# A graph layer whose adjacency is built by one-hot products: steps of one chunk instead of two, with the one-hots made on GpSimd

## The chip, the cores and the metric

One core of one Trainium2 chip runs the whole program. The metric is the device time of one execution in microseconds, as the median of the runs shown. Engines are named as in the profile: PE multiplies matrices, DVE is the vector engine, ACT the scalar engine, POOL GpSimd, SP the engine that issues DMAs.

## What is computed

x has 3125 nodes of 256 features, with 100000 edges sorted by destination. A graph attention layer and a mixture of experts follow each other, each with a residual:

```python
h = layernorm(x); q, k, v = h @ wq + bq, h @ wk + bk, h @ wv + bv
scores = sum(q[dst] * k[src], -1) / 16 + edge_weight * we + be
exp_s = exp(scores - segment_max(scores, dst)[dst])
attn = exp_s / segment_sum(exp_s, dst)[dst]
out = segment_sum(v[src] * attn[:, None], dst)
y = layernorm(h + out + h @ ws + bs) * g1 + b1
x = x + layernorm(y + gelu(y @ w_ff1 + b_ff1) @ w_ff2 + b_ff2) * g2 + b2
e = argmax(layernorm(x) @ router_w.T + router_b)         # 32 experts, 64 hidden units
x = x + relu(relu(layernorm(x) @ W1[e] + b1[e]) @ W2[e] + b2[e])
```

## The kernel before, in words

Attention is computed densely: for each tile of 125 destinations, scores against all sources, masked and weighted by an adjacency matrix A[destination, source] of summed exp(edge weight) factors. So most of the first half of the program builds A in DRAM (`adj`).

**Preparation.** 98 partitions hold 1024 edges each. DVE turns the edge weights into guarded exponents, counts at which steps each window of 5 destinations (`WIN`) begins (L989 to L991 per block of 128 steps, L1016 to L1018 per block of windows) and writes per edge a code (destination and source block, L1002) and three terms of the source's place in its block (L1003 to L1008). SP stores the last step of each window (`last_lin`, L475) and, behind that in its program, the table of edges (`edge_tab`, L484); POOL gathers the table's rows step by step (L598) and fills two rows of ones (L602); DVE makes the codes relative to their window (L1026), PE and ACT turn codes and values so that an edge of the step stands in each partition (`code_tab`, `nval_tab`, L1333 to L1341 and L757 to L765), SP stores the terms (L489) and loads them back as rows (L494). Meanwhile PE and ACT compute k, q, v and the skip part of all nodes (L1294 to L1313, L710 to L738).

**The adjacency loop** runs over 1015 steps, rounded up to 1024: 512 groups (`NG`) of 2 steps (`GROUP`), each step of 2 chunks (`SUB`) of 128 edges, all of one window; `turns` (L406) unrolls 16 groups (`BODY`) and repeats them 32 times. Per chunk, with an edge in each partition:

- PE computes the distance of the edge's place to each of 128 columns as a product of 5 bf16 rows (`distances`, L1349): (column - place) squared, less 1.
- ACT takes relu(-value x that) out of PSUM (`columns`, L778), which is the value where the column is the edge's place and 0 elsewhere (`Ys`).
- DVE compares a row of 0..124 with the code (`one_hot`, L1053), which gives for each edge a one-hot over 5 destinations x 25 source blocks (`Xs`), one instruction for two chunks.
- PE multiplies one-hot by columns (`product`, L1363, matmul at L1371, fp32), the 2 chunks of a step adding up in PSUM: a block of A of 125 x 128. An fp32 product has two records in the profile.
- DVE adds the block to the sum so far, which `keep_tab` multiplies by 1 inside a window and by 0 where one begins (`sums`, L1065, at L1081), into one of 4 buffers (`STAGES`) of `stage`. Between two add-ups stands the one-hot of a later group (L1085).
- SP stores the group's two sums to `adj` (`put`, L523), and once in 8 groups zeros to `xs_dram` (L517) and a load of the next distance rows (L495).

PE takes, per group, first the distances of two groups later, then the products. Buffers of `Xs`, `Ys` and `stage` are reused after four groups; an add-up waits for the store of four groups before (L1069).

POOL stands outside of the loop: it waits until the stores of the first tiles' rows have landed (L615) and gathers the rows of A for tiles 0 and 1 (`fetch`, L617) while the loop still runs; the others follow after it, one per tile.

**Attention**, 25 tiles: DVE turns zeros of A into a mask (`exclude`, L1104), PE computes scores in 7 blocks of columns (`front`, L1380; three fp32r products for each half of the 256 features), DVE adds the mask and takes the maximum (`guard`, L1112), ACT takes the exponent (L793), DVE multiplies by A (`weigh`, L1122), PE transposes 25 blocks and multiplies by v (`back`, L1396). The rest (FFN, routing, experts) isn't touched.

## Time and profile before

| | us |
|---|---|
| median of 3 runs | 1892.36 |
| the runs | 1892.36, 1878.16, 1903.58 |
| span of the profiled execution, first to last instruction | 1885.6 |
| busy in the span: PE, DVE, ACT, POOL | 1656.9 (88%), 1193.9 (63%), 965.5 (51%), 300.8 (16%) |

The profiled execution's time is known by its span alone; the median of the runs lies 6.8 us above it. A group of the profile is a set of instructions of one line, engine and shape, with its count, its busy time in us and the mean of one in ns, and after the second bar the idle time of the engine just before them, with what ended it. A mean of instructions that overlap is longer than the distance between their starts, so rates are read from the timeline. In a row of the chain or of the timeline the first number is the start in us and the second the duration; SPq is SP's DMA queue.

### The profile page before, as it was taken

How to read it: one execution, taken by the hardware profiler on the slowest of the kernel's cores; microseconds unless marked ns; L12 is line 12 of the kernel's file. 1: busy time of each engine (PE TensorE's matmuls, PEld its weight loads, DVE VectorE, ACT ScalarE, POOL GpSimd, SP SyncE). 2: the span in 40 equal slices, each digit the busy share in tenths (PEclk: the TensorE clock that was granted, in tenths of full speed). 3: DMA queues.
4: the chain of work that ended last, by engine and by line, in shares of the span. 5: the costliest groups of instructions: out<-in, count | busy, mean ns of one | idle time of the engine just before them, and what ended most of it. 6: DMA issues, size and time to landing. Idle time of an engine off the chain costs nothing.

```text
span 1885.6 us, 41069 instructions
## 1 busy us (share of the span) xinstructions
PE 1656.9 (88%) x11015; PEld 1378.6 (73%) x11015; DVE 1193.9 (63%) x3327; ACT 965.5 (51%) x2962; POOL 300.8 (16%) x397
## 2 busy tenths in 40 slices
PE   2898999999799999999899999999999789419960
PEld 1796888888688888887688888888888779315640
DVE  3927898988688889898555555555555578701111
ACT  1566888888588888887233333333333345103210
POOL 0022000000000000000111111111110067375435
PEclk9999999999899999999999999999999889656555
DMA  6054333333433333334822222222210100047634
GB/s 159 28 129 115 104 105 104 106 103 105 140 104 104 106 105 103 104 105 112 164 76 77 76 76 76 76 78 75 76 75 37 53 17 0 6 117 214 181 113 121
DMA packets 226999, 180.40 MB, mean 96 GB/s; under 512 B 41884, under 2 KB 218038, under 8 KB 223544
## 3 DMA queue, kind: packets, MB, share of 16 engines
q1 hardware_dynamic: 189327, 112.46, 21.6%
q0 software_dynamic: 21408, 61.20, 9.7%
q10 hardware_dynamic: 16224, 6.27, 1.5%
q8 instruction: 17, 0.28, 0.1%
q14 instruction: 23, 0.19, 0.0%
HBM read 84.94 MB, written 99.11 MB: 98 GB/s over the span
## 4 chain that ended last, share of the span: by engine, by line
PE 78%; DVE 6%; DMA 5%; POOL 4%; issue 3%; SPq 2%; ACT 1%; POOLq 0%; DVEq 0%; ACTq 0%
PE bank L1371 29%; PE bank L1404 15%; PE bank L1392 11%; PE bank L1356 9%; PE bank L1411 3%; PE bank L1486 3%; PE bank L1493 2%; PE bank L1478 2%; PE bank L1444 2%; PE bank L1436 2%; POOL arena L691 2%; POOL xs_dram L669 2%; SPq L458 1%; DMA V<-in_x 1%; DMA arena<-in_x 1%
## 5 line engine op out<-in xcount | busy, mean ns | idle before, releaser
L784 ACT ACTIVATE arena<-bank,tables 128x128 f32<-128x128 f32 x2048 | 585.2, 369 | 144.5 <-PE bank L1356 144.4
L1371 PE MATMUL bank<-arena 128*125 128x128 f32 x4096 | 585.9, 286 | 11.8 <-DVE arena L1055 11.8
L1371 PEld LDWEIGHTS bank<-arena 128*125 128x125 f32 x4096 | 488.4, 188 | 65.1 <-DVE arena L1055 11.9
L1055 DVE TENSOR_TENSOR arena<-iota_row,tables 128x250 f32<-128x250 f32 x1024 | 421.1, 412 | 0.1
L1081 DVE SCALAR_TENSOR_TENSOR arena<-arena,tables,bank 125x128 f32<-125x128 f32 x1023 | 351.9, 344 | 86.5 <-PE bank L1371 37.1
L1404 PE MATMUL bank<-V,arena 125*125 125x256 f32 x1250 | 296.4, 382 | 5.6 <-ACT arena L810 5.6
L810 ACT COPY arena<-bank 125x500 f32<-125x500 f32 (+1 forms) x175 | 90.8, 533 | 379.5 <-PE bank L1411 379.5
L1404 PEld LDWEIGHTS bank<-V,arena 125*125 125x125 f32 x1250 | 223.3, 188 | 38.0 <-ACT arena L810 10.3
L1122 DVE CUSTOM_DVE_ANT_0 arena<-arena 125x3200 f32<-125x3200 f32 x25 | 87.3, 3493 | 222.2 <-ACT arena L793 222.2
L622 POOL COPY gidx<-arow 125x1 uint32 (+1 forms) x25 | 36.4, 1455 | 1182.2 <-DVE wk_sb L1122 856.7
L1356 PE MATMUL bank<-dist_rhs,arena 5*128 5x128 bf16 x2048 | 201.6, 218 | 4.2 <-DVE tables L1039 3.4
L1356 PEld LDWEIGHTS bank<-dist_rhs,arena 5*128 5x128 bf16 x2048 | 113.8, 93 | 66.3 <-issue 4.0
L1392 PE MATMUL bank<-k_hi,q_hi 128*125 128x512 f32 (+1 forms) x350 | 137.7, 393 | 10.3 <-DVE wk_sb L1112 6.9
L1392 PE MATMUL bank<-k_lo,q_hi 128*125 128x512 f32 (+1 forms) x350 | 133.2, 380 | 0.0
L1392 PE MATMUL bank<-k_hi,q_lo 128*125 128x512 f32 (+1 forms) x350 | 133.2, 380 | 0.0
L1112 DVE CUSTOM_DVE_ANT_0 arena<-bank,arena 125x512 f32<-125x512 f32 (+1 forms) x175 | 103.0, 631 | 28.0 <-PE bank L1392 19.1
L793 ACT ACTIVATE arena<-arena,wk_sb 125x512 f32<-125x512 f32 (+1 forms) x175 | 115.8, 679 | 9.6 <-DVE wk_sb L1117 9.6
L1271 DVE TENSOR_SCALAR arena<-bank 128x256 f32<-128x256 f32 x56 | 23.7, 424 | 152.7 <-PE bank L1493 152.7
L1411 PE MATMUL bank<-ident,arena 125*125 125x125 f32 x625 | 94.5, 276 | 2.7 <-issue 2.7
L1411 PEld LDWEIGHTS bank<-ident,arena 125*125 125x125 f32 x625 | 88.7, 190 | 9.4 <-issue 3.1
L1392 PEld LDWEIGHTS bank<-k_hi,q_hi 128*125 128x125 f32 x350 | 65.9, 188 | 30.5 <-DVE wk_sb L1112 13.2
L1478 PE MATMUL bank<-ident,V 128*128 128x128 f32 x112 | 37.2, 434 | 55.1 <-DMA V<-xs_dram 55.1
(219 smaller groups left out, 1665.5 us busy)
## 6 DMA issues: line engine op xcount, KB each, us to landing
adj<-arena SPq DMA_DIRECT2D x512, 125.0 KB
xs_dram<-zeros SPq DMA_DIRECT2D x64, 112.0 KB, 3.2
V<-xs_dram SPq DMA_DIRECT2D x56, 128.0 KB, 2.3
ys_dram<-arena SPq DMA_DIRECT2D x56, 128.0 KB, 1.9
w_dram<-in_L_ffn_W SPq DMA_DIRECT2D x2, 2048.0 KB
V<-in_x SPq DMA_DIRECT2D x5, 625.0 KB
q_dram<-arena ACTq DMA_DIRECT2D x25, 125.0 KB, 2.3
wq_sb<-q_dram SPq DMA_DIRECT2D x25, 125.0 KB, 7.8
```

Source lines behind the costliest of these rows:

```text
L784: ins = nc.scalar.activation(Ys[:, q, k, :], bank[2 + s][:, k * LO:(k + 1) * LO], ACT.Relu, scale=nval_tab[:, bass.ds(i, 1)])
L793: ins = nc.scalar.activation(Z[0:TILE, s, c:c + n], Z[0:TILE, s, c:c + n], ACT.Exp, bias=nmax[:, s:s + 1])
L810: nc.scalar.copy(PT[0:TILE, s, j:j + n, :], bank[4 + g % 2][0:TILE, 0:n * TILE].rearrange("p (n d) -> p n d", n=n)).then_inc(pt_ready, 1)
L1055: ins = V_.tensor_tensor(Xs[:, s, cols, :], iota_row[:, 0:TILE].unsqueeze(1).to_broadcast([P, SUB, TILE]), code_tab[:, bass.ds(g * GC + k ...
L1081: ins = V_.scalar_tensor_tensor(stage[0:TILE, q, k, :], prev, keep_tab[0:TILE, bass.ds(g * GROUP + k, 1)], ps, ALU.mult, ALU.add)
L1112: V_.tensor_tensor_reduce(out=Z[0:TILE, s, c:c + n], in0=bank[b % 4][0:TILE, 0:n], in1=Z[0:TILE, s, c:c + n], scale=1.0, scalar=-BIG, op0= ...
L1122: V_.tensor_tensor_reduce(out=Z[0:TILE, s, :], in0=Z[0:TILE, s, :], in1=A_sb[0:TILE, s, :], scale=1.0, scalar=0.0, op0=ALU.mult, op1=ALU.a ...
L1356: ins = mm(bank[2 + s][:, k * LO:(k + 1) * LO], dist_rows[:, j // LOADG, c:c + CHUNK], dist_rhs[:, :], start=True, stop=True)
L1371: ins = mm(o, Xs[:, j % STAGES, k, :], Ys[:, j % STAGES, k, :], start=(k % SUB == 0), stop=(k % SUB == SUB - 1))
L1392: ins = mm(bank[b % 4][0:TILE, 0:n], q[:, s, k, :], v[:, k, j, :].rearrange("p j l -> p (j l)"), start=(i == 0), stop=(i == len(parts) - 1))
L1404: ins = mm(bank[6 + s][0:TILE, 0:D], PT[0:TILE, s, j, :], V[:, j, :], start=(j == 0), stop=(j == NT - 1))
L1411: ins = tr(bank[4 + g % 2][0:TILE, j * TILE:(j + 1) * TILE], Z[0:TILE, s, (j0 + j) * LO:(j0 + j) * LO + TILE], ident[0:TILE, 0:TILE])
```

## The change

`SUB` goes from 2 to 1: a step has one chunk, so there are 1406 steps, rounded up to 1408, in 704 groups of 2 steps (44 turns of 16), and a product is complete after one matmul. The tables in preparation grow with it: 11 blocks of 128 steps for 8 (`SBLK`), 784 columns for 392 in the counts (`NS`), one gather per block for two.

A source is now block x 131 + place: 24 blocks of 131 places (`HI`, `LO`) instead of 25 of 128 columns with 125 used. The one-hot has 120 columns, a block of A is 120 x 131, its row 3144 numbers, and scores are computed in 7 blocks of 448 columns.

The two distance products of a group take their 5 rows from different strips of 32 partitions (`STRIP`), into different banks (`dist_bank`); the rows are loaded by two DMAs, and two fills of POOL write the ones.

The one-hots are made by POOL, one tensor_scalar per chunk with the code as a scalar per partition, from copies of 16 codes (`held`); only the last group of every eight (`OWN`) is made by DVE in one instruction. POOL's gathers for attention stand behind its whole loop. PE's wait for the sums of four groups earlier, which lay in the order of DVE's instructions before, is now written out.

The core of the diff:

```diff
-SUB = 2
+SUB = 1
...
-LO = 128
-ROW = NT * LO
+HI, LO = 24, 131
+ROW = HI * LO
+MW = WIN * HI
+KB = 448
+NCOL = 7 * KB
 DIST = 5
+STRIP = 32
...
-ZROWS = MT * P // (2 * TURNS)
+ZROWS = -(-MT * P // (2 * TURNS * 12)) * 12
...
-SCH = [(c, min(512, ROW - c)) for c in range(0, ROW, 512)]
+SCH = [(c, KB) for c in range(0, NCOL, KB)]
...
-        with nc.sbuf_tensor("kT", [P, KH, NT, LO], F32) as kT, nc.sbuf_tensor("tables", [P, KH * ROW], F32) as tables:
+        with nc.sbuf_tensor("kT", [P, KH, NCOL], F32) as kT, nc.sbuf_tensor("tables", [P, KH * NCOL], F32) as tables:
...
-        Xs = view(STAGES * GC * TILE).rearrange("p (s k m) -> p s k m", s=STAGES, k=GC)
+        Xs = view(STAGES * GC * MW).rearrange("p (s k m) -> p s k m", s=STAGES, k=GC)
...
+        HELD = LOADG * GC
+        LOADW = LOADG * CHUNK
+        dist_rows = view(LOADW)[0:(GC - 1) * STRIP + DIST, :].bitcast(BF16).rearrange("p (s c) -> p s c", s=2)
...
+        OWN = LOADG - 1
+        def pool_groups(j, i):
+            return i * (BODY - 2) + j - j // LOADG
+        def dist_bank(s, k):
+            return bank[2 + s + 4 * k]
...
-                sp.dma_start(dist_rows[2:DIST, s, :], term_rows.ap().rearrange("c i e -> c (i e)")[
-                    :, bass.ds(n * LOADW, LOADW)]).then_inc(rows_in[s], 16)
+                for k in range(GC):
+                    sp.dma_start(dist_rows[k * STRIP + 2:k * STRIP + DIST, s, :].rearrange("c (i e) -> c i e", e=CHUNK),
+                                 term_rows.ap().rearrange("c (i k) e -> c k i e", k=GC)[
+                                     :, k, bass.ds(n * LOADG, LOADG), :]).then_inc(rows_in[s], 16)
...
-                             stage[0:TILE, j % STAGES, :, :]).then_inc(stored[j % STAGES], 16)
+                             stage[0:MW, j % STAGES, :, :]).then_inc(stored[j % STAGES], 16)
...
-            nc.gpsimd.memset(dist_rows[0:2, :, :], 1.0).then_inc(ones_set, 1)
+                        bass.IndirectOffsetOnAxis(ap=cidx[:, u, b:b + 1], axis=0)).then_inc(gath_in[b // 2], 16)
+            pool.wait_ge(ws_set, KH + 1)
+            for k in range(GC):
+                if k:
+                    pool.wait_ge(ones_set, k)
+                nc.gpsimd.memset(dist_rows[k * STRIP:k * STRIP + 2, :, :], 1.0).then_inc(ones_set, 1)
...
+            pool.wait_ge(ones_set, GC)
+            pool.wait_ge(tab_set, SBLK)
+            pool.wait_ge(terms_stored, 16 * SUB * SBLK)
+            def hold_codes(n, h):
+                nc.gpsimd.tensor_copy(held[:, h, :], code_tab[:, bass.ds(n * HELD, HELD)]).then_inc(codes_held, 1)
+            hold_codes(0, 0)
+            def one_hots(g, j, i):
+                h = j // LOADG
+                if j % LOADG == 0:
+                    pool.wait_ge(codes_held, 2 * i + h + 1)
+                if j % LOADG == 2 and not (isinstance(i, int) and i == TURNS - 1 and h):
+                    wait_from(pool, x_ready, pool_groups(j, i) - 2)
+                    hold_codes(2 * i + h + 1, 1 - h)
+                if j % LOADG == OWN:
+                    return
+                wait_from(pool, prod_done, g - STAGES + 1)
+                pool.sem_inc(pool_mark, 1)
+                for k in range(GC):
+                    c = j % LOADG * GC + k
+                    ins = nc.gpsimd.tensor_scalar(Xs[:, j % STAGES, k, :], iota_row[:, 0:MW], held[:, h, c:c + 1], None,
+                                                  ALU.is_equal)
+                ins.then_inc(x_ready, 1)
+            turns(pool, one_hots)
...
-                    ins = nc.scalar.activation(Ys[:, q, k, :], bank[2 + s][:, k * LO:(k + 1) * LO], ACT.Relu,
+                    ins = nc.scalar.activation(Ys[:, q, k, :], dist_bank(s, k)[:, 0:LO], ACT.Relu,
...
-            od(V_.scalar_tensor_tensor(codes_o, chunked(dstf), float(NT), chunked(hi_e[:, 0:EROW]), ALU.mult, ALU.add))
-            od(V_.scalar_tensor_tensor(srcf, hi_e[:, 0:EROW], -float(TILE), srcf, ALU.mult, ALU.add))
+            rounded(hi_e[:, 0:EROW], srcf, 1.0 / LO, 0.5 / LO - 0.5)
+            od(V_.scalar_tensor_tensor(codes_o, chunked(dstf), float(HI), chunked(hi_e[:, 0:EROW]), ALU.mult, ALU.add))
...
-            def one_hot(g, s, k):
-                cols = slice(k * SUB, (k + 1) * SUB)
-                ins = V_.tensor_tensor(Xs[:, s, cols, :], iota_row[:, 0:TILE].unsqueeze(1).to_broadcast([P, SUB, TILE]),
-                                       code_tab[:, bass.ds(g * GC + k * SUB, SUB)].unsqueeze(2).to_broadcast([P, SUB, TILE]),
-                                       ALU.is_equal)
-                if k == GROUP - 1:
-                    ins.then_inc(x_ready, 1)
-            for g in range(STAGES - 1):
-                for k in range(GROUP):
-                    one_hot(g, g, k)
...
-                    prev = stage[0:TILE, q, k - 1, :] if k else stage[0:TILE, (q - 1) % STAGES, GROUP - 1, :]
-                    ps = product_bank(j)[0:TILE, k * LO:(k + 1) * LO]
+                    prev = stage[0:MW, q, k - 1, :] if k else stage[0:MW, (q - 1) % STAGES, GROUP - 1, :]
+                    ps = product_bank(j)[0:MW, k * LO:(k + 1) * LO]
                     if first:
-                        ins = V_.tensor_copy(stage[0:TILE, q, k, :], ps)
+                        ins = V_.tensor_copy(stage[0:MW, q, k, :], ps)
                     else:
-                        ins = V_.scalar_tensor_tensor(stage[0:TILE, q, k, :], prev,
-                                                      keep_tab[0:TILE, bass.ds(g * GROUP + k, 1)], ps, ALU.mult, ALU.add)
+                        ins = V_.scalar_tensor_tensor(stage[0:MW, q, k, :], prev,
+                                                      keep_tab[0:MW, bass.ds(g * GROUP + k, 1)], ps, ALU.mult, ALU.add)
                     ins.then_inc(sum_ord if k < GROUP - 1 else sums_ready, 1)
-                    if not (isinstance(i, int) and i == TURNS - 1 and j > BODY - STAGES):
-                        one_hot(g + STAGES - 1, (q - 1) % STAGES, k)
+                if j % LOADG == OWN - STAGES + 1:
+                    V_.tensor_tensor(Xs[:, OWN % STAGES, :, :], iota_row[:, 0:MW].unsqueeze(1).to_broadcast([P, GC, MW]),
+                                     code_tab[:, bass.ds((g + STAGES - 1) * GC, GC)].unsqueeze(2).to_broadcast([P, GC, MW]),
+                                     ALU.is_equal).then_inc(own_x_ready, 1)
...
-                mm(bank[0][:, 0:NS], ones[0:PP, :], s_diag, start=True, stop=True).then_inc(rows_bc, 1)
+                mm(bank[0][:, 0:512], ones[0:PP, :], s_diag[:, 0:512], start=True, stop=True)
+                mm(bank[1][:, 0:NS - 512], ones[0:PP, :], s_diag[:, 512:NS], start=True, stop=True).then_inc(rows_bc, 1)
...
-                    pe.wait_ge(rows_in[j // LOADG], 16 * loads)
+                    pe.wait_ge(rows_in[j // LOADG], 16 * GC * loads)
+                c = j % LOADG * CHUNK
                 for k in range(GC):
-                    c = ((j % LOADG) * GC + k) * CHUNK
-                    ins = mm(bank[2 + s][:, k * LO:(k + 1) * LO], dist_rows[:, j // LOADG, c:c + CHUNK], dist_rhs[:, :],
+                    rows_ = slice(k * STRIP, k * STRIP + DIST)
+                    ins = mm(dist_bank(s, k)[:, 0:LO], dist_rows[rows_, j // LOADG, c:c + CHUNK], dist_rhs[rows_, :],
...
-                pe.wait_ge(x_ready, g + 1)
+                if j % LOADG == OWN:
+                    pe.wait_ge(own_x_ready, 2 * i + j // LOADG + 1)
+                else:
+                    pe.wait_ge(x_ready, pool_groups(j, i) + 1)
+                wait_from(pe, sums_ready, g - STAGES + 1)
+                wait_from(pe, sums_ready, g - STAGES + 1)
                 for k in range(GC):
-                    o = product_bank(j)[0:TILE, k // SUB * LO:(k // SUB + 1) * LO]
+                    o = product_bank(j)[0:MW, k // SUB * LO:(k // SUB + 1) * LO]
...
-                        ins = mm(bank[b % 4][0:TILE, 0:n], q[:, s, k, :], v[:, k, j, :].rearrange("p j l -> p (j l)"),
+                        ins = mm(bank[b % 4][0:TILE, 0:n], q[:, s, k, :], v[:, k, c:c + n],
```

## Rows read from the trace of the kernel before

**Rows 1.** Stages: us; PE, PEld, DVE, ACT, POOL busy; granted clock, DMA share, GB/s.

```profile
158.60:889.40 730.80, 716.54 (x6136) 601.45 (x6136) 640.92 (x2047) 585.64 (x2048) 3.25 (x4) 0.99 0.37 106
889.40:1484.00 594.60, 577.15 (x2925) 489.44 (x2925) 317.41 (x699) 202.67 (x379) 63.74 (x46) 0.99 0.25 78
...
1640.00:1885.00 245.00, 132.65 (x448) 81.66 (x448) 39.17 (x70) 41.18 (x112) 128.56 (x162) 0.53 0.50 145
```

**Rows 2.** Timeline of one period of the loop; start us, us, engine, operation.

```profile
700.12 0.39 PE L1356 MATMUL bank<-dist_rhs,arena 5*128 5x128 bf16 x4
...
700.45 1.14 PE L1371 MATMUL bank<-arena 128*125 128x128 f32 x8
700.53 0.35 DVE L1081 SCALAR_TENSOR_TENSOR arena<-arena,tables,bank 125x128 f32<-125x128 f32 x1 [0.30 <-PE bank L1371]
...
700.79 0.41 DVE L1055 TENSOR_TENSOR arena<-iota_row,tables 128x250 f32<-128x250 f32 x1
701.12 0.34 DVE L1081 SCALAR_TENSOR_TENSOR arena<-arena,tables,bank 125x128 f32<-125x128 f32 x1
...
701.52 0.39 PE L1356 MATMUL bank<-dist_rhs,arena 5*128 5x128 bf16 x4
```

**Rows 3.** DVE groups: adding up, one-hot, and two that wait on the one before.

```profile
L1055 DVE TENSOR_TENSOR arena<-iota_row,tables 128x250 f32<-128x250 f32 x1024 | 421.1, 412 | 0.1
L1081 DVE SCALAR_TENSOR_TENSOR arena<-arena,tables,bank 125x128 f32<-125x128 f32 x1023 | 351.9, 344 | 86.5 <-PE bank L1371 37.1 <-DMA adj<-arena 14.7
...
L1131 DVE RECIPROCAL wk_sb<-wk_sb 125x1 f32<-125x1 f32 x25 | 4.1, 164 | 0.9
```

**Rows 4.** POOL: groups by shape, and one instruction of its timeline.

```profile
L650 POOL TENSOR_TENSOR wk_sb<-wk_sb,minus_half 125x1 f32<-125x1 f32 x50 | 29.5, 589 | 9.2 <-POOL wk_sb L647 9.2
...
L589 POOL TENSOR_TENSOR ws_sb<-ws_sb,ident 128x128 f32<-128x128 f32 x2 | 0.9, 454 | 14.1 <-DMA bq_col<-in_L_gnn_bq 14.1
...
L590 POOL TENSOR_SCALAR_AFFINE_SELECT before<-before 128x128 f32<-128x128 f32 x1 | 0.3, 294 | 0.0
...
1543.17 0.22 POOL L647 TENSOR_SCALAR wk_sb<-wk_sb 125x1 f32<-125x1 f32 x1
```

**Rows 5.** The store of one group: its issue, its transfer's window, and another store's landing.

```profile
162.48 5.46 SPq L523 DMA_DIRECT2D adj<-arena  x4
...
163.30:164.90 1.60, 1.60 (x15) 1.37 (x15) 0.98 (x4) 0.66 (x3) 0.00 (x0) 0.92 0.29 80
...
ys_dram<-arena SPq DMA_DIRECT2D x56, 128.0 KB, 1.9
```

**Rows 6.** The stall in the loop: the chain, and the gather on POOL before it.

```profile
481.65 17.52 DMA adj<-arena
...
479.26 1.47 POOL L625 DMA_INDIRECT arena<-adj,gidx  x1 [1.00 <-POOL gidx L622]
```

**Rows 7.** Preparation: timelines of DVE and of SP's queue, and POOL's gathers as a group.

```profile
75.46 0.43 DVE L990 TENSOR_SCALAR arena<-arena,step_col 128x392 f32<-128x392 f32 x1
75.92 0.56 DVE L991 TENSOR_REDUCE cnt<-arena 128x1 f32<-128x392 f32 x1
...
103.74 0.26 SPq L475 DMA_DIRECT2D last_lin<-wrow  x1
...
146.95 5.86 DVE L1026 TENSOR_SCALAR arena<-arena,wneg 128x256 f32<-128x256 f32 x2 [2.27 <-DMA arena<-edge_tab,cidx]
...
L598 POOL DMA_INDIRECT arena<-edge_tab,cidx x16 | 15.5, 969 | 111.8 <-DMA edge_tab<-arena 107.2 <-issue 4.6
```

**Rows 8.** The turn into attention: POOL's gathers, DVE's first masking, one front.

```profile
arena<-adj,gidx POOLq DMA_INDIRECT x25, 15.8
...
896.41 1.82 DVE L1104 TENSOR_SCALAR arena<-arena 125x3200 f32<-125x3200 f32 x1
...
1118.47 9.02 PE bank L1392 x42
```

**Rows 9.** PE at the other clock, at the start of the loop.

```profile
162.00 1.88 PE L1371 MATMUL bank<-arena 128*125 128x128 f32 x8
```

More of the change, by code:

```diff
@@ L153, in gnn_moe @@
         x1 = sb("x1", [TILE, NT, D])
-        ARENA = 19050
+        ARENA = 19260
         arena = sb("arena", [P, ARENA])
@@ L176, in gnn_moe @@
         assert SBLK * SUB * TABW <= edges_only
-        cmp_o = view(4 * P)
-        s_row, o_row, iota_c = view(4 * P), view(4 * P), view(4 * P)
-        cmp_s, s_row, o_row, iota_c = (v[:, 0:NS] for v in (cmp_o, s_row, o_row, iota_c))
+        cmp_o = view(NS)
+        s_row, o_row, iota_c = view(NS), view(NS), view(NS)
+        cmp_s = cmp_o
         diag_flat = view(SBLK * P)
@@ L295, in gnn_moe @@
             "code_set", "idx_set", "rel_set", "tabT_done", "tab_set", "keep_set"))
-        gath_in = [sem(f"gath_in{b}") for b in range(SBLK)]
+        s_copied, codes_held, own_x_ready = sem("s_copied"), sem("codes_held"), sem("own_x_ready")
+        gath_in = [sem(f"gath_in{b}") for b in range(-(-SBLK // 2))]
+        gathered = [16 * min(2, SBLK - 2 * b) for b in range(-(-SBLK // 2))]
         last_set, last_stored, last_in, arow_set = (sem(n) for n in ("last_set", "last_stored", "last_in", "arow_set"))
@@ L329, in gnn_moe @@
         x_t = x.rearrange("(t p) d -> p t d", p=TILE)
-        xs_v, ys_v = (v.ap().rearrange("(j p) d -> p j d", p=P) for v in (xs_dram, ys_dram))
+        xs_v, ys_v = (v.ap()[0:MT * P, :].rearrange("(j p) d -> p j d", p=P) for v in (xs_dram, ys_dram))
         out_t = out.rearrange("(t p) d -> p t d", p=TILE)
@@ L609, in _ @@
             pool.wait_ge(q_stored[1], 16 * (NT // 2))
+            pool.wait_ge(ones_set, GC)
[15 more added lines that the diff above has]
+                pool.sem_inc(pool_mark, 1)
+                for k in range(GC):
+                    c = j % LOADG * GC + k
[3 more added lines that the diff above has]
+            turns(pool, one_hots)
             last_group = (2 * TILE // WIN + NS - 2) // GROUP
@@ L799, in key_parts @@
                 c, n = SCH[b]
-                j = slice(c // LO, (c + n) // LO)
-                nc.scalar.copy(k_hi[:, :, j, :], kT[:, :, j, :]).then_inc(k_hi_set, 1)
+                nc.scalar.copy(k_hi[:, :, c:c + n], kT[:, :, c:c + n]).then_inc(k_hi_set, 1)
             def weights(t, s, t_next, u):
@@ L939, in _ @@
             i1 = iota_row[0:1, :]
-            od(V_.tensor_tensor(cmp_o[0:1, 0:P], i1, i1, ALU.mult))
-            rounded(cmp_o[0:1, P:2 * P], cmp_o[0:1, 0:P], 1.0 / P, 0.0)
-            od(V_.tensor_scalar_mul(dist_line[:, 0, :], cmp_o[0:1, P:2 * P], float(P)))
-            od(V_.scalar_tensor_tensor(dist_line[:, 1, :], cmp_o[0:1, 0:P], -1.0, dist_line[:, 0, :], ALU.add, ALU.subtract))
+            lo_sq, lo_sqh = cmp_o[0:1, 0:LO], cmp_o[0:1, LO:2 * LO]
+            od(V_.tensor_tensor(lo_sq, i1, i1, ALU.mult))
+            rounded(lo_sqh, lo_sq, 1.0 / P, 0.0)
+            od(V_.tensor_scalar_mul(dist_line[:, 0, :], lo_sqh, float(P)))
+            od(V_.scalar_tensor_tensor(dist_line[:, 1, :], lo_sq, -1.0, dist_line[:, 0, :], ALU.add, ALU.subtract))
             od(V_.tensor_copy(dist_line[:, 2, :], i1))
@@ L996, in _ @@
             od(V_.tensor_tensor(wneg[:, :], cnt[:, :], step_col[:, :], ALU.subtract))
[L997 removed]
+            od(V_.tensor_scalar_mul(wneg[:, :], wneg[:, :], float(WIN * HI)))
             chunked = lambda ap: ap.rearrange("p (k e) -> p k e", k=PC)
             od(V_.tensor_copy(srcf, si))
[L1001 to L1003 removed]
+            rounded(hi_e[:, 0:EROW], srcf, 1.0 / LO, 0.5 / LO - 0.5)
+            od(V_.scalar_tensor_tensor(codes_o, chunked(dstf), float(HI), chunked(hi_e[:, 0:EROW]), ALU.mult, ALU.add))
+            od(V_.scalar_tensor_tensor(srcf, hi_e[:, 0:EROW], -float(LO), srcf, ALU.mult, ALU.add))
             od(V_.tensor_scalar_mul(terms_o[:, :, 0, :], chunked(srcf), -2.0))
@@ L1095, in key_rest @@
                 c, n = SCH[b]
-                j = slice(c // LO, (c + n) // LO)
                 dve.wait_ge(k_hi_set, b + 1)
-                V_.tensor_tensor(k_lo[:, :, j, :], kT[:, :, j, :], k_hi[:, :, j, :].bitcast(F32), ALU.subtract).then_inc(k_split, 1)
+                V_.tensor_tensor(k_lo[:, :, c:c + n], kT[:, :, c:c + n], k_hi[:, :, c:c + n].bitcast(F32),
+                                 ALU.subtract).then_inc(k_split, 1)
             def exclude(t, s, u):
@@ L1103, in exclude @@
                 wait_from(dve, tr_ready, len(TRG) * (t - 1))
-                V_.tensor_scalar(Z[0:TILE, s, :], A_sb[0:TILE, s, :], 0.0, -BIG, ALU.is_equal, ALU.mult).then_inc(excluded, 1)
+                V_.tensor_scalar(Z[0:TILE, s, :], A_sb[0:TILE, s, 0:NCOL], 0.0, -BIG, ALU.is_equal, ALU.mult).then_inc(excluded, 1)
             def guard(t, s, u):
```

56 lines of the change are left out of this document (27 added, 29 removed).

## The prediction

> **What bounds the kernel now.** I read the page first, then the busy time by stage. The adjacency loop (from 158.6 to 889.4 us) is the largest stage with 730.8 us, in which PE is busy for 716.5, DVE for 640.9, ACT for 585.6 and POOL for 3.3; attention follows with 594.6, and what comes after it takes 1885.6 - 1484.0 = 401.6 us [rows 1]. The change rebuilds the loop, so I then read one period of it. PE starts distances at 700.12 and again at 701.52: 1.39 to 1.40 us per group, with nothing between PE's pieces. Four distances take 0.33 (0.082 each) and eight product records 1.06 (0.133 each; a product has two records). DVE starts an add-up, a one-hot 0.26 later and the next add-up 0.33 after that, so its two pairs need 1.18 of the 1.39: PE bounds the loop, and DVE hides its waits behind one-hots [rows 2]. 512 x 1.392 = 713 us; the other 18 are one stall of 17.5 us, after POOL's gathers for the first attention tiles had started inside the loop and the stores of the loop waited for the same DMA engines [rows 6].
>
> **The loop after.** A chunk of 128 edges is now a step of its own: ceil(100000/128) + 624 = 1406 steps instead of 1015, rounded up to 704 groups of 2 chunks where there were 512 groups of 4. I cost one group on every engine.
>
> PE: 2 products are 4 records of 0.133 (131 columns for 128 add about 2%, 120 rows of weights for 125 take something off) = 0.53; 2 distances at 0.082 = 0.16, or about 0.10 if the two row strips run beside each other, which no row shows. 0.63 to 0.70, I take 0.69 [rows 2]. That is 486 us against 713: PE is no longer what is late.
>
> DVE: it still adds up twice, each add-up reading the sum before it. An add-up takes 0.344 [rows 3]. So far a one-hot stood between two of them; now the second comes at once and waits for the first. The nearest row of an instruction that waits for the one just before on DVE idles 0.9/25 = 0.036 us (L1131) [rows 3]. So 2 x (0.347 + 0.036) = 0.77. In one group of eight DVE builds the one-hots itself: 0.33 of distance between starts [rows 2], or 0.41 and a wait for POOL's reads on top, say 0.7; 0.04 to 0.09 per group. DVE: 0.80 to 0.86. Below that only if the waits cost nothing.
>
> POOL: 14 tensor_scalars of 120 columns per 8 groups, an operation that the trace doesn't show at this width. Bounds: with one column it takes 0.22; at 128 columns a compare-and-select of one input takes 0.29 and a two-input operation 0.454, so 0.29 to 0.45 [rows 4]. Each of ours reads a column of scalars beside its input, so I go above the one-input row: 0.40. To this come one copy of codes per 8 groups with a wait of POOL on itself (9.2/50 = 0.18 in the row of L650) and the waits of 7 groups at about 0.1: 1.1 in all. (14 x 0.40 + 1.1)/8 = 0.84; with the bounds 0.65 and 0.93 [rows 4].
>
> Stores: a group's sums leave in one DMA and their buffer is reused four groups later. Before, the first store was issued at 162.48 and moved data from 163.30 to 164.90, with 0.29 of 16 engines busy: five engines, 1.6 us. Another store of the same size, 128 partitions, lands in 1.9 from its issue [rows 5]. A split into equal parts explains both (125 into 5, 128 into 16), and 120 partitions split into 15. I take 1.9: the buffer comes back after 0.77 + 0.03 + 1.9 + 0.1 = 2.8 us for 4 groups, 0.70 each. At five engines it would be 1.5 each, a rival below. The Trainium skill ("DMA: Bandwidth & Descriptors", why a DMA increments its semaphore by 16) says that a DMA runs on the largest number up to 16 that divides the slowest dimension. By that rule 125 gives 5, with which this trace's 0.29 agrees, and 120 gives 15, which no row here shows.
>
> ACT has 2 activations where it had 4 in 1.14 us: about 0.63 and not on the path.
>
> So DVE (0.80 to 0.86) and POOL (0.84) are close together, with the stores and PE at 0.70. Engines that near each other wait for each other at times: I take 0.87 per group. 704 x 0.87 = 612 us, and no gathers inside the loop, so no stall like that of [rows 6].
>
> DVE beside POOL is the place where a page would say otherwise. In preparation, two additions of DVE on 128 x 256 (L1026) took 5.86 us, while POOL filled the rows of ones (L602) [rows 7]; an add-up of half as many columns takes 0.344 [rows 3]. The Trainium skill ("SBUF — State Buffer", who interferes with whom) says that the pair of ports shared by DVE and POOL is an exclusive lock, but that a DVE instruction with one SBUF input outside the two-port modes doesn't need it. By that rule the add-ups (one input in PSUM) stay at 0.344 beside POOL, and only the DVE one-hots wait; if they too were blocked for half of POOL's 0.40 each, a group would take 1.17.
>
> **Preparation.** DVE's chain grows. Counting takes 0.43 + 0.56, 1.06 per block with gaps [rows 7]; with 784 columns for 392 I put 1.63, and 11 blocks for 8: 17.9 - 8.5 = +9.4. The same pair five times over windows +2.9, the rest about +2. This moves last_lin and then the edge table, which stands behind it in SP's program (last_lin leaves at 103.74) [rows 7], by some 14 us. Then 11 gathers instead of 16 at (15.5 + 4.6) / 16 = 1.26 us each: -6 [rows 7]; and POOL's fill, 2 x 2048 columns for 8192, blocks L1026 for less: -3. Net +5 (0 to +12): the loop starts at 163.6.
>
> **Into attention.** POOL issued the first two gathers inside the loop; now it reaches them behind its last one-hots, about 1 us before the loop's end. A gather lands in 15.8, and here two go at once beside SP's weight copies, so 19 to 22. Masking of tile 0 started 7.2 us after the loop (896.41) [rows 8], and would start at about 20: +12 (8 to 18). Score columns go from 3200 to 3136: 2% of the 9.02 us of a front [rows 8], -5 over 25 tiles. Attention: 594.6 + 12 - 5 = 601.6. What follows it: 401.6, unchanged.
>
> **Sum.** 163.6 + 612 + 601.6 + 401.6 = 1779 us of span. The profiled span is 1885.6 and the median 1892.36; I add the 7 between them: **1786 us**, 5.6% below. A measurement of this kernel tells about 2% from no change: faster is below 1854.5, slower above 1930.
>
> **Rivals.** Each is 1167 + 704 x (time per group) + 7.
>
> *POOL becomes the bound and the kernel slower.* Every product needs POOL's one-hots, seven groups of eight. A tensor_tensor of POOL with a single column takes 0.589 (L650) [rows 4], so a price far above 0.40 isn't excluded. At 0.60 each, (8.4 + 1.1)/8 = 1.19 and 2012 us. It decides from 0.54 (1.08 per group). Against it: 0.22 for one column of this very operation. Chance 0.09.
>
> *The stores stay on five engines* (for: nothing shows a 120-partition store): 1.5 per group, 2230 us. Chance 0.03.
>
> *No gain that can be told.* POOL at 0.48 to 0.53; or the 524-byte pieces, which no longer start on multiples of 512, cost double; or PE's clock. PE would be busy for 0.69 of 0.87. In the experts' stage it is busy for 132.7 of 245 us at a granted 0.53 [rows 1]; at half clock eight records took 1.88 us instead of 1.14 [rows 2, 9], so a group's 0.69 becomes 1.14, and a quarter of the loop there costs 0.27 x 176 = 48 us. About 1.03 per group, 1899. Chance 0.09.
>
> *Better than my sum.* POOL near 0.30 and DVE's waits on itself partly free, so that PE and the stores are next: 0.75, 1702. For: DVE's starts overlap ends by 0.09 where it needn't wait [rows 2]. Chance 0.20.
>
> The forecast has 0.59, its own range 1740 to 1850. The range for 8 in 10 takes in half of the better case and some of the case without gain: 1705 to 1885. Faster 0.59 + 0.20 = 0.79, same 0.09, slower 0.12.
>
> **What would show it.** Right: a loop of 590 to 640 us with 0.84 to 0.91 per group; PE with gaps ended by DVE or POOL; DVE's two add-ups 0.38 apart; POOL's operation at 0.35 to 0.45; stores over 0.4 of the DMA engines; the loop's start within 159 to 171; the first masking some 20 us after the loop. Wrong: POOL's operation above 0.5, or add-ups that grow beyond 0.40 beside POOL; DVE waiting mostly for stores; a granted clock below 0.9 in the loop.

## The result, and the profile after it

The kernel after takes **2144.84 us** (median of 4 runs, 2134.45 to 2161.55), the kernel before 1895.07 beside it: ratio **1.134, 95% interval 1.126 to 1.142**. The forecast was 1786 with a range of 1705 to 1885, so it was wrong in size and in sign. The profiled execution took 2135.78 with a span of 2134.1; the one of before had a span of 1885.6, so 248.5 us are to be found.

The same view as in [rows 1], of the kernel after: the loop, attention, and what follows it.

```profile
165.30:1135.30 970.00, 968.87 (x4215) 713.62 (x4216) 521.07 (x1492) 444.54 (x1409) 714.21 (x1321) 0.50 0.40 100
1135.30:1752.70 617.40, 573.45 (x2934) 503.99 (x2934) 316.99 (x704) 202.50 (x380) 66.85 (x49) 0.98 0.25 80
1752.70:2134.10 381.40, 232.05 (x1259) 178.57 (x1257) 155.99 (x390) 102.97 (x313) 207.22 (x312) 0.73 0.35 102
```

The loop takes 970.0 us where [rows 1] had 730.8: +239. Attention has +23 and what follows it -20. The loop starts at 165.3 instead of 158.6. The loop is the whole story, and its row says two things. PE is busy in 968.9 of 970.0 us, and its granted clock is 0.50 from one end to the other: 1.2 GHz, where the kernel before ran its loop at 0.99.

One period of the loop, from the timeline of the kernel after, to be held against [rows 2]:

```profile
700.96 0.10 PEld L1404 LDWEIGHTS bank<-dist_rhs,arena 5*128 5x128 bf16 x2 [0.25 <-ACT arena L837]
700.96 0.29 PE L1404 MATMUL bank<-dist_rhs,arena 5*128 5x131 bf16 x2
701.18 1.23 PE L1424 MATMUL bank<-arena 128*120 128x131 f32 x4
701.19 0.85 DVE L1124 SCALAR_TENSOR_TENSOR arena<-arena,tables,bank 120x131 f32<-120x131 f32 x2 [0.53 <-PE bank L1424]
701.23 1.14 POOL L659 TENSOR_SCALAR arena<-iota_row,arena 128x120 f32<-128x120 f32 x2 [0.24 <-PE bank L1424]
...
702.34 0.29 PE L1404 MATMUL bank<-dist_rhs,arena 5*128 5x131 bf16 x2
```

From 700.96 to 702.34 is 1.38 us for two chunks; the kernel before took 1.40 for four. DVE and POOL both wait for PE's bank. So do they in the groups:

```profile
L1424 PE MATMUL bank<-arena 128*120 128x131 f32 x2816 | 863.8, 462 | 0.1
L659 POOL TENSOR_SCALAR arena<-iota_row,arena 128x120 f32<-128x120 f32 x1232 | 701.4, 581 | 253.9 <-PE bank L1424 241.1 <-issue 3.8 <-POOL arena L642 0.2
...
L1124 DVE SCALAR_TENSOR_TENSOR arena<-arena,tables,bank 120x131 f32<-120x131 f32 x1407 | 494.4, 351 | 447.2 <-PE bank L1424 343.4 <-DVE arena L1124 26.3
L837 ACT ACTIVATE arena<-bank,tables 128x131 f32<-128x131 f32 x1408 | 444.4, 367 | 525.4 <-PE bank L1404 525.4
```

Every other engine idles for PE. Yet POOL's operation takes 0.581, over the 0.54 from which I had let it bind: had PE been fast, there was a second thing in line. Stores land in 2.3 us (the page's row of issues: 704 of 122.8 KB), and no engine waits for one.

### The profile page after: what moved, and what is told of

It is laid out like the page before. It is cut to its first block, busy times and chain, and to the rows that moved or that the text cites. A ratio compares the mean times of both kernels' runs of the same rounds, so it can differ in the third digit from the quotient of the medians.

```text
span 2134.1 us, 41927 instructions
## 1 busy us (share of the span) xinstructions
PE 1882.0 (88%) x9089; PEld 1491.0 (70%) x9089; DVE 1085.7 (51%) x2792; ACT 823.5 (39%) x2328; POOL 1006.3 (47%) x1713
## 4 chain that ended last, share of the span: by engine, by line
PE 78%; DVE 5%; DMA 5%; POOL 4%; issue 4%; SPq 2%; ACT 1%; DVEq 0%; POOLq 0%; ACTq 0%
PE bank L1424 38%; PE bank L1455 13%; PE bank L1443 9%; PE bank L1404 7%; PE bank L1462 3%; PE bank L1495 2%; PE bank L1487 2%; PE bank L1537 2%; POOL xs_dram L722 1%; POOL arena L744 1%; PE bank L1544 1%; SPq L476 1%; DMA arena<-adj,gidx 1%; DMA V<-in_x 1%; PE bank L1529 1%
## 5 line engine op out<-in xcount | busy, mean ns | idle before, releaser
L1424 PE MATMUL bank<-arena 128*120 128x131 f32 x2816 | 863.8, 462 | 0.1
L659 POOL TENSOR_SCALAR arena<-iota_row,arena 128x120 f32<-128x120 f32 x1232 | 701.4, 581 | 253.9 <-PE bank L1424 241.1
L1124 DVE SCALAR_TENSOR_TENSOR arena<-arena,tables,bank 120x131 f32<-120x131 f32 x1407 | 494.4, 351 | 447.2 <-PE bank L1424 343.4
L1424 PEld LDWEIGHTS bank<-arena 128*120 128x120 f32 x2816 | 642.7, 311 | 83.3 <-POOL arena L659 0.3
L837 ACT ACTIVATE arena<-bank,tables 128x131 f32<-128x131 f32 x1408 | 444.4, 367 | 525.4 <-PE bank L1404 525.4
L1404 PE MATMUL bank<-dist_rhs,arena 5*128 5x131 bf16 x1408 | 203.6, 287 | 4.4 <-DVE tables L1094 3.5
L1443 PE MATMUL bank<-k_hi,q_hi 128*125 128x448 f32 x350 | 136.7, 390 | 35.5 <-DVE wk_sb L1157 32.4
L1443 PE MATMUL bank<-k_lo,q_hi 128*125 128x448 f32 x350 | 130.0, 371 | 0.0
L1443 PE MATMUL bank<-k_hi,q_lo 128*125 128x448 f32 x350 | 129.7, 371 | 0.0
L846 ACT ACTIVATE arena<-arena,wk_sb 125x448 f32<-125x448 f32 x175 | 114.4, 671 | 23.7 <-DVE wk_sb L1162 23.7
## 6 DMA issues: line engine op xcount, KB each, us to landing
adj<-arena SPq DMA_DIRECT2D x704, 122.8 KB, 2.3
```

The source lines that it names most:

```text
L659: ins = nc.gpsimd.tensor_scalar(Xs[:, j % STAGES, k, :], iota_row[:, 0:MW], held[:, h, c:c + 1], None, ALU.is_equal)
L837: ins = nc.scalar.activation(Ys[:, q, k, :], dist_bank(s, k)[:, 0:LO], ACT.Relu, scale=nval_tab[:, bass.ds(i, 1)])
L846: ins = nc.scalar.activation(Z[0:TILE, s, c:c + n], Z[0:TILE, s, c:c + n], ACT.Exp, bias=nmax[:, s:s + 1])
L1124: ins = V_.scalar_tensor_tensor(stage[0:MW, q, k, :], prev, keep_tab[0:MW, bass.ds(g * GROUP + k, 1)], ps, ALU.mult, ALU.add)
L1404: ins = mm(dist_bank(s, k)[:, 0:LO], dist_rows[rows_, j // LOADG, c:c + CHUNK], dist_rhs[rows_, :], start=True, stop=True)
L1424: ins = mm(o, Xs[:, j % STAGES, k, :], Ys[:, j % STAGES, k, :], start=(k % SUB == 0), stop=(k % SUB == SUB - 1))
```

## The experiments

All variants are of the kernel after unless said otherwise. Each was executed once, but for the last two, whose numbers are medians of 4 and 6 runs. A time per group comes from a window of 400 us inside the loop, by its PE records (6 per group of two chunks, 12 per group of four). The kernel before took 1864.55 us beside the first four experiments, 1904.79 beside e_own4_pad, e_own4_pad_nochain and e_before_pad, 1886.25 beside e_nopool_pad, e_nopool_pad_nochain and e_imm, and 1908.41 beside e_both. Totals of different sets can therefore differ by some 2% without a cause in the kernel, and the argument goes by the time per group.

**Who holds the loop: POOL?** (e_nopool) After the first eight groups POOL compares one column of one chunk per group. The adjacency is left out by it.

```diff
-for k in range(GC):
-    nc.gpsimd.tensor_scalar(Xs[:, j % STAGES, k, :], iota_row[:, 0:MW], held[:, h, c:c + 1], ...)
+for k in range(GC - 1 if few else 0, GC):
+    nc.gpsimd.tensor_scalar(Xs[:, j % STAGES, k, 0:m], iota_row[:, 0:m], held[:, h, c:c + 1], ...)   # m = 1
```

> The changed kernel with POOL's one-hots left out: after the first eight groups each group of POOL writes one column of one chunk instead of two chunks of 120 columns, so its 1.16 us per group fall to about 0.22 and A is not computed. Theory PE alone: PE's own pieces (0.23 per product record at the half clock, and a stop of about 0.25 and 0.12 each time it goes from products to distances and back) make the 1.38 us per group, and the granted clock stays at 0.5 whatever POOL does: loop still 1.38 per group, 970 us. Theory POOL: POOL's 0.581 us per one-hot held PE back and so took its clock: without it the granted clock is 1.0 and a group takes 0.80 to 0.90, loop 560 to 630 us.

Measured: 2136.26 us, granted clock of the loop 0.50, still 1.38 us per group. POOL's group now waits almost all the time:

```profile
L661 POOL TENSOR_SCALAR arena<-iota_row,arena 128x1 f32<-128x1 f32 (+1 forms) x623 | 180.7, 291 | 774.1 <-PE bank L1426 770.8 <-issue 3.0 <-POOL arena L642 0.2
```

POOL is off the path: PE alone sets the loop. (The row also prices the operation: 0.28 to 0.29 us for one column.)

**Every second group's one-hots on DVE** (e_own4) instead of every eighth (`OWN = (1, 3, 5, 7)`, put between a group's two add-ups):

> The changed kernel with every second group's one-hots on DVE (1, 3, 5, 7 of eight), set between its two add-ups, and the others on POOL. POOL then needs (8 x 0.581 + 0.5)/8 = 0.65 per group. Theory PE alone: still 1.38 per group at clock 0.5. Theory POOL: 0.90 to 1.00 per group at full clock, loop 630 to 700 us.

Measured: 2158.54 us, 0.50, 1.38 us per group. Taking work from POOL and giving it to DVE changes nothing, which agrees with the first.

**Without row strips** (e_nostrip): both distance products use rows 0 to 4 of the array, and their inputs come in one load again.

> The changed kernel with both distance products of a group in the same strip of partitions, loaded by one DMA as in the kernel before; banks as in the changed kernel. If the strips cause the stops or the low clock: a group falls below 1.38 and the clock rises. If not (which both other theories say): 1.36 to 1.42 per group, clock 0.5.

Measured: 2236.89 us. PE in the timeline of this kernel:

```profile
700.79 0.40 PE L1397 MATMUL bank<-dist_rhs,arena 5*128 5x131 bf16 x2
701.11 1.23 PE L1417 MATMUL bank<-arena 128*120 128x131 f32 x4
702.27 0.40 PE L1397 MATMUL bank<-dist_rhs,arena 5*128 5x131 bf16 x2
```

The period is 1.48 and the two distances take 0.40 instead of 0.29. I had expected 1.36 to 1.42, so that missed: the strips do run beside each other, and save 0.10 us per group at this clock. That part of the change is a gain. The granted clock is 0.50 here too.

**Distances over all 128 rows of the array** (e_pad). The rows that carried nothing now hold zeros on one side, so that distances and products have the array in the same shape.

```diff
-mm(dist_bank(s, k)[:, 0:LO], dist_rows[rows_, j // LOADG, c:c + CHUNK], dist_rhs[rows_, :], ...)
+mm(dist_bank(s, k)[:, 0:LO], dist_rows[:, j // LOADG, c:c + CHUNK], dist_rhs[:, k, :], ...)   # zeros outside strip k
```

> The changed kernel with its distance products made over all 128 partitions (zeros outside of the five rows), so that distances and products use the array in the same shape; everything else as it was. Theory PE alone: the stops between the two kinds of product go, PE is dense even at the half clock (about 1.13 per group), the granted clock rises to 1.0 and POOL becomes the bound: (14 x 0.581 + 0.5) / 8 = 1.08 to 1.12 per group, loop 760 to 790 us. Theory POOL: nothing changes on POOL, so the clock stays at 0.5; a group takes 1.13 to 1.38. Rival that the stops are the fill of the array and not its shape: unchanged 1.38.

Measured: 1967.71 us, 168 to 177 below the kernel after; 1.13 us per group. Work was added to the matrix engine's operands, not taken, and the loop became 0.25 us per group shorter. PE's timeline at the loop's start has both clocks:

```profile
169.99 0.43 PE L1406 MATMUL bank<-tables,arena 128*128 128x131 bf16 x2
170.21 1.17 PE L1426 MATMUL bank<-arena 128*120 128x131 f32 x4
171.18 0.43 PE L1406 MATMUL bank<-tables,arena 128*128 128x131 bf16 x2
...
173.28 0.28 PE L1406 MATMUL bank<-tables,arena 128*128 128x131 bf16 x2
173.58 0.71 PE L1426 MATMUL bank<-arena 128*120 128x131 f32 x4
...
176.48 0.28 PE L1406 MATMUL bank<-tables,arena 128*128 128x131 bf16 x2
176.59 0.66 PE L1426 MATMUL bank<-arena 128*120 128x131 f32 x4
177.09 0.28 PE L1406 MATMUL bank<-tables,arena 128*128 128x131 bf16 x2
```

and a window of its loop (columns as in [rows 1]):

```profile
200.00:600.00 400.00, 292.24 (x2118) 255.14 (x2118) 260.41 (x750) 220.85 (x706) 357.12 (x667) 0.89 0.48 122
```

Before the clock rose (169.99 to 171.18) a group took PE 1.19, against 1.38 with 5-row distances at the same clock: **0.19 us per group went with the change of shape**. The padded distances no longer run beside each other, so the kernel without strips is the nearer partner, and against its 1.48 it is 0.29. Then the granted clock rose, and where nothing holds PE a group takes it 0.61 (176.48 to 177.09), about half of 1.19. In the mean of the window the clock was 0.89, so PE was at half clock for part of it. What is late next stands in the waits of this kernel (engine, line, waited for: us, times, longest), from 200 to 900 us:

```profile
DVE arena L1127 <- DVE arena L1127: 126.0, 542, 0.5
PE bank L1426 <- DVE arena L1131: 125.1, 77, 2.1
POOL arena L662 <- PE bank L1426: 72.9, 91, 1.9
...
PE bank L1426 <- POOL arena L662: 10.5, 28, 0.6
```

and in DVE's timeline:

```profile
701.31 0.35 DVE L1127 SCALAR_TENSOR_TENSOR arena<-arena,tables,bank 120x131 f32<-120x131 f32 x1 [0.15 <-DVE arena L1127]
701.92 0.35 DVE L1127 SCALAR_TENSOR_TENSOR arena<-arena,tables,bank 120x131 f32<-120x131 f32 x1 [0.25 <-DVE arena L1127]
702.42 0.35 DVE L1127 SCALAR_TENSOR_TENSOR arena<-arena,tables,bank 120x131 f32<-120x131 f32 x1 [0.15 <-DVE arena L1127]
```

An add-up that waits for the one before starts 0.15 us after its end within a group and 0.25 at a group's turn: 2 x 0.35 + 0.40 = 1.10 per group. PE's largest wait is for the one-hot that DVE makes once in eight groups (L1131): PE waits for an engine that is behind. I had expected POOL as the next bound and a clock of 1.0. POOL (busy for 357 of 400 us here) was near too, so four kernels take them apart.

**Half of POOL's work gone, on top of the padding** (e_own4_pad: the edits of e_own4 and e_pad together, but with one fill of ones for all rows of the array in place of e_pad's three fills):

> The kernel after with the padded distances of e_pad, and every second group's one-hots on DVE (between the two add-ups of a group) instead of every eighth. If after the padding POOL's two comparisons of 0.58 to 0.59 us per group bound the loop of e_pad (1.14 us per group), half of them leave POOL and the loop falls to 0.90 to 1.00 us per group: 1820 to 1890 us. If DVE's chain of add-ups does (each waits for the sum before it: starts 0.50 to 0.61 us apart in e_pad, so 1.10 us per group), the loop stays at 1.08 to 1.18 us per group: 1940 to 1990 us, and the wait of the add-up for the add-up before it stays the largest idle time of DVE.

Measured: 2004.67 us, 15 above my range, and 1.16 us per group: no gain from POOL's relief. The add-up's wait for the add-up before it is still DVE's largest (90.4 us of 203.9 between 200 and 900 us), and PE waits 226.4 us there for one-hots that DVE makes. That these lengthen the loop from 1.13 to 1.16 is likely, but it is a difference of single executions.

**The chain of add-ups cut as well** (e_own4_pad_nochain: `prev = zeros[0:MW, 0:LO]` and no wait between add-ups; the running sum is left out):

> As e_own4_pad, but each add-up takes zeros in place of the previous sum and waits for none: the running sum is left out. DVE-chain theory: the loop falls by over 0.1 us per group against e_own4_pad, to what PE takes at full clock, 0.80 to 0.95 us: 1800 to 1860 us, granted clock of the loop 0.9 or more. Rival (POOL, or the array itself): within 20 us of e_own4_pad.

Measured: 1919.46 us, 1.055 us per group. The chain held it, by 0.10 us per group as expected, but the end that I gave (0.80 to 0.95) was missed: something at 1.05 took over. DVE's group in this kernel from 200 to 900 us:

```profile
L1133 DVE SCALAR_TENSOR_TENSOR arena<-zeros,tables,bank 120x131 f32<-120x131 f32 x1324 | 418.2, 347 | 200.7 <-DMA adj<-arena 162.0 <-PE bank L1431 31.8 <-issue 0.5
```

DVE now waits for the store that empties the buffer it is to write.

**POOL's work cut to one column, on top of the padding** (e_nopool_pad; adjacency left out), and then **the chain cut too** (e_nopool_pad_nochain):

> e_pad with POOL's comparisons cut to one column of one chunk after the first eight groups (the adjacency is not computed). If the chain of add-ups on DVE holds the loop of e_pad at 1.125 us per group, the loop stays at 1.05 to 1.13 us and the total at 1910 to 1970 us. If POOL's comparisons do (2 x 0.59 us in seven of eight groups, 1.03 us, and the buffers' turnaround), it falls to 0.85 to 1.00 us per group: 1780 to 1880 us.

> e_nopool_pad and no add-up waits for the one before it (zeros in its place, the running sum is left out): what is left is PE, two ACT operations, two DVE operations of 0.35 us and the stores. PE alone: 0.80 to 0.90 us per group, 1740 to 1810 us. Stores (DVE waited 162 us for them in e_own4_pad_nochain at 1.05 us per group): 1.00 to 1.05 us, about 1880 to 1920 us, DMA share above 0.5 and the add-up's wait for the store the largest of DVE's.

Measured: 1967.44 us and 1.12 per group for the first, the same as with all of POOL's work (1967.71); 1920.86 us and 1.06 for the second. The group of the second from 200 to 900 us:

```profile
L1125 DVE SCALAR_TENSOR_TENSOR arena<-zeros,tables,bank 120x131 f32<-120x131 f32 x1326 | 401.7, 348 | 276.2 <-DMA adj<-arena 199.5 <-PE bank L1424 70.5 <-issue 0.7
```

So once PE is out of the way DVE's chain is the bound, at 1.12; behind it stand the stores, at 1.05 to 1.06; POOL, at (14 x 0.59 + 1.1)/8 = 1.17 by my own way of counting, is not: with all of its work in e_pad a group takes 1.13, and PE waits for POOL for 10.5 of 700 us. That count is too high. Whether POOL with all of its work would hold a loop at 1.05 no run shows. An estimate for the stores: with four store buffers and a landing of 2.9 us (median of this kernel; 2.3 in the kernel after) a buffer comes back after some 0.35 + 0.35 + 0.33 + 2.9 = 3.9 us, or 0.98 each. That is an argument from durations; more buffers were not tried, so the stores as the bound at 1.05 are read from DVE's waits and not shown by an edit.

**What POOL's 0.581 is made of** (e_imm). A constant stands in place of the code that each partition reads (A is wrong by it).

> The kernel after with a constant in place of the code that POOL's comparison reads for each partition (the adjacency is wrong by it). Asks what of the 0.581 us of a 128x120 comparison is the operand: if it is the operand, 0.40 to 0.45 us; if it is the comparison itself, 0.56 to 0.59 us. The total stays within 20 us of the kernel after (2145 us) by the theory that PE at half clock alone sets the loop.

Measured: 2134.25 us, the operation 0.507 (median) instead of 0.581. The total says again that POOL isn't on the path. The operand costs 0.07, not the 0.18 by which my 0.40 was off, and 0.507 lies in neither of the two ranges expected. With 0.283 for a single column (the median in the kernel without POOL's work), the other 119 add 0.30: 2.5 ns each.

**The kernel before with its distances over 128 rows** (e_before_pad). If the shape of the array costs this much, the kernel before pays it too.

```diff
-dist_rows = view(LOADW)[0:DIST, :].bitcast(BF16)
+dist_rows = view(LOADW)[:, :].bitcast(BF16)          # 128 rows, filled with ones
-dist_rhs = sb("dist_rhs", [DIST, LO], BF16)
+dist_rhs = tables[:, 5 * SLOTS:5 * SLOTS + LO // 2].bitcast(BF16)   # rows past the fifth zero
```

> The kernel before with its four distance products over 128 rows of the array (rows past the fifth meet zeros) instead of 5. If each change between 5 and 128 rows stops PE, as in the kernel after, two stops of 0.11 us per group go: PE falls from 1.39 to about 1.17 us per group, and DVE (1.18 us per group by its three operations) is the next bound: loop 1.20 to 1.28 us per group, total 1800 to 1850 us, ratio to the kernel before 0.95 to 0.975. If DVE or the stores over 125 partitions bind already at 1.37, or the stops have another cause: ratio 0.99 to 1.01.

Measured: 1839.08 us, ratio 0.968 (0.961 to 0.975). Total and ratio are as expected; the loop is not, 1.33 us per group instead of 1.20 to 1.28. At its start, with one-hots made ahead, PE runs twelve periods of 1.15 us in a row; later there are periods of 1.20 between longer ones:

```profile
173.71 0.39 PE L1359 MATMUL bank<-tables,arena 128*128 128x128 bf16 x4
173.93 1.09 PE L1374 MATMUL bank<-arena 128*125 128x128 f32 x8
174.86 0.39 PE L1359 MATMUL bank<-tables,arena 128*128 128x128 bf16 x4
...
600.33 0.39 PE L1359 MATMUL bank<-tables,arena 128*128 128x128 bf16 x4
...
601.78 0.39 PE L1359 MATMUL bank<-tables,arena 128*128 128x128 bf16 x4
...
602.00 1.14 PE L1374 MATMUL bank<-arena 128*125 128x128 f32 x8
...
602.98 0.39 PE L1359 MATMUL bank<-tables,arena 128*128 128x128 bf16 x4
```

173.71 to 174.86 is 1.15: 0.22 until the products start and 0.93 until the next distances, where [rows 2] had 0.33 and 1.07. So two stops of 0.11 and 0.14 per group are gone, 0.24 to 0.25 in all, at full clock on both sides. 601.78 to 602.98 is 1.20 (0.22 and 0.98); there DVE, which needs 1.18 for its four operations, no longer leaves PE that pace. 600.33 to 601.78 is 1.45. The first store leaves at 174.8 instead of 162.5, and e_both has the same at 175.3. POOL's fill isn't what is late:

```profile
145.75 6.94 POOL L605 MEMSET arena<- 128x8192 bf16 x1
```

Over two rows it took 6.91 us and started at 145.49. What is late is PE's part of the preparation: from 135.9 to 149 us its instructions for q, k and v start one at a time, many after about 1 us of idle time for which the trace names no releaser. Why stays open. In the loop DVE waits for stores, 63 times between 200 and 800 us:

```profile
L1084 DVE SCALAR_TENSOR_TENSOR arena<-arena,tables,bank 125x128 f32<-125x128 f32 x908 | 312.6, 344 | 45.9 <-DMA adj<-arena 31.8 <-PE bank L1374 10.3 <-issue 0.2
```

**The same with the source blocks of the change** (e_both), 24 of 131, so that a store covers 120 partitions; steps stay at two chunks, and all one-hots on DVE. Attention and the stores of zeros are those of the change too, since they depend on the blocks.

```diff
-LO = 128
-ROW = NT * LO
+HI, LO = 24, 131
+ROW = HI * LO
+MW = WIN * HI
 ...
-    stage[0:TILE, j % STAGES, :, :]).then_inc(stored[j % STAGES], 16)
+    stage[0:MW, j % STAGES, :, :]).then_inc(stored[j % STAGES], 16)
```

> e_before_pad (steps of two chunks, one-hots on DVE, distances over 128 rows) with the source blocks of the kernel after: 24 blocks of 131, so that a store covers 120 partitions. Asks whether stores over 125 partitions are what keeps e_before_pad at 1.32 us per group instead of the 1.20 of its undisturbed periods. If they are: 1.20 to 1.24 us per group, waits for the adj store under 10 us, loop 615 to 635 us, total 1780 to 1810 us, ratio to the kernel before 0.935 to 0.955. If PE and DVE hold it (DVE busy 92% of the loop): 1.30 to 1.33 us per group, 1825 to 1850 us, ratio 0.96 to 0.975.

Measured: **1798.37 us, ratio 0.946 (0.940 to 0.951)**, faster than both kernels and as expected. The loop's stores run from 175.3 to 801.0, 1.22 us per group. The same group of this kernel, in the same 600 us as that of e_before_pad:

```profile
L1094 DVE SCALAR_TENSOR_TENSOR arena<-arena,tables,bank 120x131 f32<-120x131 f32 x980 | 342.0, 349 | 18.5 <-DMA adj<-arena 12.1 <-PE bank L1384 5.7 <-issue 0.5
```

Two waits for a store instead of 63, one of them 10.5 us long, where POOL's gathers start as in [rows 6]. The waits for a store sum to 12.1 us, a little over the 10 that I had set. The DVE operations are all but the same length (0.349 and 0.402 instead of 0.344 and 0.413), so what kept the kernel with padded distances from 1.20 was the store over 125 partitions.

## Why the prediction was wrong

**PE's price in the loop (0.63 to 0.70, "I take 0.69").** This is the term that failed: a group cost PE 1.38, and PE alone set the loop. By the runs 1.38 is 0.61 for the work at full clock, as dense padded groups of e_pad show, about 0.58 more for the half clock (1.19 there), and 0.19 for the change of shape, net of what the strips save. So two things were missing, and the larger is the clock.

**The stops.** I divided one period of before into 0.33 for four distances and 1.06 for eight products, and halved each. But the 0.33 and the 1.07 between starts in [rows 2] each hold a stop: with distances over 128 rows they are 0.22 and 0.93. So 0.24 of the 1.39 belongs to no product: it is paid once per group, when PE goes from 5-row to 128-row operands and back. A change that makes groups half as long pays it twice as often. The Trainium skill ("TensorEngine Tiling (Array Packing)", Key Properties) says that changing the tiling mode drains the engine. The runs agree with that in so far as both padded pairs lose time per group, 0.24 us in the kernel before at full clock and 0.29 against the kernel without strips at half clock. They show the price and that it hangs on the number of rows; which mode the array was in no record says, and that section of the Trainium skill gives no price. I had not weighed it.

**PE's clock.** The 0.69 is a price at full clock; half clock stood only in the rival "no gain", which gave PE 1.14 for a group and let a quarter of the loop run there, 48 us. The price was 1.38 and the share was all of it. By the rows: in the kernel before, the loop also began at half clock ([rows 9]) and rose to full some microseconds later. In the kernel after, PE sits at 0.50 from 160 us to the loop's end while its records fill 968.9 of 970.0 us; the kernels without strips, without POOL's work, with DVE's one-hots and with the constant do the same. In the seven kernels with padded distances it was full at the loop's start or within some 20 us of it, and its mean from 200 to 600 us lay between 0.89 and 0.99. A busy PE in the records is thus no sign of a granted clock. What separates the two sets is the 5-row distance once per two chunks. That the padding gives the clock back is shown; why the chip grants less without it is not settled by these runs. The two effects are entangled: 0.19 of the 0.25 us per group that the padding gave back is the shape at half clock, and the rest is the clock, cut off by DVE's chain.

**DVE (0.80 to 0.86).** Wrong, and hidden by PE: with PE fast this term alone would have taken the forecast out of its range. The wait of an add-up for the sum before it costs 0.15 within a group and 0.25 at the turn, not the 0.036 that I took from the row of L1131 in [rows 3]. That row is a mean over 25 instructions of one column elsewhere in the kernel. Width isn't the reason: L1137 of before, on 256 columns and also waiting for the instruction in front of it, idles 0.9/25 as well. Why an add-up of the loop waits longer stays open; no row of before shows two of them in a row. The chain alone needs 1.10 to 1.12 per group. So the change would not have been faster than the kernel before even with PE out of the way: e_pad, in which PE waits for DVE, is at 1967.71 against 1864.55 for the kernel before beside it.

**POOL (0.40 each, 0.84 per group).** The operation takes 0.581, twice the 0.29 of the one-input row in [rows 4] and near the 0.589 of the row that I named in the rival. The rival's price was right; its conclusion (POOL binds and the kernel is slower, 2012 us) was not, as the runs without POOL's work show. The Trainium skill ("GPSIMD Engine Reference", Engine selection) calls one-input operations on it roughly line-rate. This comparison took 2.5 ns for each added column, and 0.581/120 = 4.8 ns with its fixed part, where DVE's one-hot took 0.402/240 = 1.7 with its own. So the measurement differs from that sentence, and it decides here.

**Port contention.** DVE's add-up stayed at 0.351 beside POOL. Right. DVE's one-hot, which by the rule in the prediction would wait for POOL, took 0.402 (the longest of 88 took 0.502), as in e_both, where POOL has no one-hots. So no run shows that wait.

**Stores.** The split held. The first store of the kernel after moved its data from 169.9 to 170.7 us, with 0.63 of the DMA engines busy (0.82 in the busiest 0.2 us), where the first of before took 1.6 us at 0.29 ([rows 5]):

```profile
169.90:170.70 0.80, 0.80 (x6) 0.80 (x4) 0.57 (x2) 0.63 (x2) 0.80 (x3) 0.50 0.63 157
```

So more than five engines carry it; 15 of them fit, and so does e_both against e_before_pad. It lands in 2.3 us, not 1.9. That stores can't bind was wrong, though: 0.70 each left out that a landing grows to 2.9 when they come closer, and 1.05 is what they allow.

**The ends.** Loop start 165.3 against 163.6: the preparation's sum was near. Attention 617.4 against 601.6: the gather is now issued behind POOL's last one-hots and lands late, as the chain of waits of the kernel after shows:

```profile
1132.64 0.58 POOL arena L659
1133.23 0.14 POOL gidx L675
1133.41 1.99 issue
1135.40 23.13 DMA arena<-adj,gidx
1158.55 1.81 DVE arena L1149
```

Masking starts 23 us after the loop; I had 20, from the 7.2 of before, and the 16 us that this adds is most of the +22.8. The fewer score columns were to give back 5 us and did not show. What follows attention fell by 20.2 us, to 381.4, and I had it unchanged. Its granted clock is 0.73 against 0.66 in the same stretch of before, and the busy times of POOL and DVE are the same. In the other kernels with this change the stretch took 377 us at 0.73 (e_imm) to 405 at 0.64 (e_nostrip), so it is the execution's clock and no merit of the change.

By terms, for the profiled execution: 2135.8 - 1786 = 350 us, of which the loop is 970 - 612 = 358, its start 2, attention 16, what follows it -20, and the time around the span -5 (1.7 instead of 7).

## What to carry to other kernels

Where PE alternates between operands of few rows and of 128, count the alternations, not only the products: each costs a stop that smaller groups multiply, and zeros in the unused rows can take it away. A price of PE read at full clock holds only if the new loop is granted that clock: a changed pattern of products can lose it for a whole stage, so half clock belongs in the forecast as a case of its own. Read a chain of dependent instructions by the distance between starts where nothing stands between them; if the kernel before always had something in between, its price isn't in the trace and needs bounds. And a store's number of partitions decides how many DMA engines it fills: 120 can beat 125.
